# Counts in the sort, edge weights in groups of 64 rows, attributes four quads ahead, and root products inside the relational loops

## What is computed

```python
def _rgcn_layer(x, src, dst, edge_type, edge_attr, W, root, bias, nn_w, nn_b):
    n = x.shape[0]
    edge_w = edge_attr @ nn_w.T + nn_b          # 53125 x 32 by 32 x 256
    msg = jax.nn.relu(x[src] * edge_w)
    out = x @ root + bias
    for r in range(N_REL):                      # 3 relations
        mask = edge_type == r
        m = jnp.where(mask[:, None], msg, 0.0)
        s = jax.ops.segment_sum(m, dst, num_segments=n)
        cnt = jax.ops.segment_sum(mask.astype(x.dtype), dst, num_segments=n)
        mean = s / jnp.maximum(cnt, 1.0)[:, None]
        out = out + mean @ W[r]
    return out
```

## Time and profile before

| | |
|---|---|
| median of 3 runs | 5542.0 us (5537.71 to 5550.64) |
| the profiled execution | 5537.87 us, span 5536.0 us |
| mean granted TensorE clock | 0.814 of full speed |
| busy: PE, PEld | 3725.7 us (67%), 2918.2 us (53%) |
| busy: DVE, ACT, POOL | 2873.2 us (52%), 1521.7 us (27%), 2684.7 us (48%) |
| sort loop | 24 to 650 us of the span |
| relational loops | 2872 to 3679, 3782 to 4551 and 4663 to 5427 us |
| dense stages | 3679 to 3775, 4555 to 4651 and 5427 to 5516 us |

### The profile page before, as it was taken

How to read it: one execution, slowest core, us unless ns; L and a number is a source line. 1 busy time by engine, 2 the same in 40 slices (tenths; PEclk the granted TensorE clock), 3 DMA queues, 4 the chain that set the end, 5 groups by cost and what they waited for, 6 DMA issues and landing times.

```text
span 5536.0 us, 114152 instructions
## 1 busy us (share of the span) xinstructions
PE 3725.7 (67%) x28769; PEld 2918.2 (53%) x28769; DVE 2873.2 (52%) x10883; ACT 1521.7 (27%) x3922; POOL 2684.7 (48%) x2864
## 2 busy tenths in 40 slices
PE   2212185666666766666658888997778778777778
PEld 1111133444444344444437777876666677666677
DVE  5444454444445544444465555554555554555556
ACT  1000003555554155555522222211222221222220
POOL 5666504555554255555545455424555533555550
PEclk6555587989888899888867888898788889888888
DMA  2111136666665366666632222212222321222220
GB/s 46 22 22 22 21 116 187 174 172 174 170 169 120 104 173 173 171 172 171 167 102 79 77 83 78 80 50 81 81 81 83 85 65 58 84 83 81 81 83 30
DMA packets 375435, 563.79 MB, mean 102 GB/s; under 512 B 133583, under 2 KB 261632, under 8 KB 375362
## 3 DMA queue, kind: packets, MB, share of 16 engines
q0 software_dynamic: 155264, 442.19, 29.5%
q1 hardware_dynamic: 165304, 113.92, 7.3%
q10 hardware_dynamic: 54794, 6.81, 0.8%
HBM read 521.54 MB, written 41.08 MB: 102 GB/s over the span
## 4 chain that ended last, share of the span: by engine, by line
PE 35%; issue 18%; DVE 16%; another core or an unknown queue 16%; DVEq 6%; SPq 4%; DMA 3%; ACT 2%; ACTq 0%; POOL 0%; POOLq 0%
PE bank L1074 10%; PE bank L1089 9%; PE bank L963 5%; PE bank L1030 3%; SPq L783 2%; DVE ht L1640 2%; PE bank L1040 2%; DVE region L1724 2%; DVE ht L1627 1%; PE bank L1013 1%; DVEq L651 1%; PE bank L1056 1%; DVE region L1650 1%; DMA rings<-edge_attr_T 1%
## 5 line engine op out<-in xcount | busy, mean ns | idle before, releaser
L555 POOL DMA_INDIRECT gring<-h_rows,gidx x1248 | 1185.6, 950 | 1078.3 <-DVE rings L1701 734.7
L1089 PE MATMUL bank<-rings 128*128 128x96 f32 x6168 | 1041.5, 314 | 216.8 <-DVE region L1724 142.4
L1074 PE MATMUL bank<-nnwt,rings 128*128 128x256 f32 x3084 | 1001.2, 452 | 218.9 <-DMA rings<-edge_attr_T 153.0
L1089 PEld LDWEIGHTS bank<-rings 128*128 128x128 f32 x6168 | 965.9, 226 | 313.2 <-DVE region L1724 187.5
L1701 DVE TENSOR_TENSOR rings<-bank,gring 128x256 f32<-128x256 f32 x1542 | 583.0, 420 | 952.0 <-remote 417.5
L1156 ACT ACTIVATE rings<-rings 128x512 f32<-128x512 f32 x771 | 485.6, 630 | 1864.0 <-DVE rings L1701 1491.5
L1074 PEld LDWEIGHTS bank<-nnwt,rings 128*128 128x128 f32 x3084 | 626.6, 225 | 311.4 <-DMA rings<-edge_attr_T 145.3
L1030 PE MATMUL bank<-rings 128*64 128x128 f32 x4096 | 393.1, 320 | 541.1 <-ACT rings L1189 202.6
L523 POOL DMA_INDIRECT gring<-kv_rows,gidx x512 | 487.9, 953 | 473.0 <-PE bank L1056 185.4
L523 POOL DMA_INDIRECT ht<-kv_rows,gidx x512 | 493.7, 964 | 417.5 <-PE bank L1056 229.6
L1724 DVE TENSOR_TENSOR region<-region,bank 128x192 f32 x1542 | 539.2, 350 | 123.8 <-issue 27.2
(11 more groups left out here) (245 smaller groups left out, 4702.4 us busy)
## 6 DMA issues: line engine op xcount, KB each, us to landing
rings<-node_in_window_T SPq DMA_DIRECT2D x256, 128.0 KB
rings<-edge_attr_T SPq DMA_DIRECT2D x1548, 16.0 KB
gring<-h_rows,gidx POOLq DMA_INDIRECT x1248
kv_rows<-rows SPq DMA_DIRECT2D x50, 258.0 KB, 2.5
gring<-kv_rows,gidx POOLq DMA_INDIRECT x512
ht<-kv_rows,gidx POOLq DMA_INDIRECT x512
region<-edge_records SPq DMA_DIRECT2D x13, 576.0 KB, 7.0
edge_records<-rings POOLq DMA_INDIRECT x416
```

Of the source, the lines that this page charges most:

```text
L555: g.indirect_dma_start(out=gring_r[:, 2 * u + k, :], out_offset=None, in_=h_d[l], in_offset=bass.IndirectOffsetOnAxis(ap=gidx_r[:, half, 2 ...
L1074: ins = pe.matmul(bank[slot % RL][:, k * D:(k + 1) * D], eat[:, b, 2 * (slot % 2) + k, :], nnwt[:, :], start=True, stop=True)
L1089: ins = pe.matmul(b[:, (2 * k + c) * SEG:(2 * k + c + 1) * SEG], prod[:, slot % RL, (2 * k + c) * P:(2 * k + c + 1) * P], one, start=True, ...
```

## The change

Four edits go together.

1. **Counts in the sort.** `one_hot` makes a second one-hot of the segment (relation and node in the window, 96 wide), and `ranks` multiplies it by the first in four products a group, added up in bank 4 over all 104 groups. The sums by segment and window are the counts. The count products, the adds and `ones_f` leave layer 0.
2. **Edge weights in groups of 64 rows.** The even tile of a pair lies in partitions 0 to 63 of `eat`, the odd in 64 to 127, the weights `nnwt` in both, and each product contracts over its own 64. The four products of a quad are issued together, the two groups in different banks.
3. **Attributes four quads ahead.** `eat` holds four quads (`EB`) in the space of two.
4. **Root products in the loops.** In the first 25 trips of a loop SP fetches a block of rows (`hrow`), PE transposes it (bank 6), ACT copies it, PE multiplies it by the root weights (bank 7) and ACT keeps the result in `rootrows`. The dense stage has six products a block, no transposes and no `copy_features`. The message sums have two banks in place of four (`RS`), and `LAG_RACC` goes from 3 to 2.

```diff
@@ sort: ranks, one_hot
+                for c in range(CG):
+                    pe.matmul(bank[4][0:SEG, 0:NW], onehot_s[:, slot, :, c], onehot_w[:, slot, c, :],
+                              start=isinstance(trip, int) and g + c == 0, stop=isinstance(trip, int) and g == G - 1 and c == CG - 1)
...
-                                iota_w[:, :, :], ALU.is_equal).then_inc(s_ohw, 1)
+                                iota_w[:, :, :], ALU.is_equal)
+                v.tensor_tensor(onehot_s[:, slot, :, :],
+                                own_f[:, bass.ds(g * CG, CG)].unsqueeze(1).to_broadcast([EP, SEG, CG]),
+                                iota_w[:, 0:SEG, :], ALU.is_equal).then_inc(s_ohw, 1)
@@ SP, loop of a layer
+                    if root and u == U_LOAD:
+                        wait_freed(sp, s_turn, l * NT + trip)
+                        sp.dma_start(hrow, h_d[l][bass.ds(trip * P, P), :]).then_inc(s_hrow, 16)
...
-                    wait_freed(sp, s_ew, l * RPAIRS + trip * U + u - 2)
+                    wait_freed(sp, s_ew, l * RQUADS + trip * QTRIPS + quad - EB + 1)
@@ PE, dense stage
-                    for r in range(-1, NREL):
-                        o = bank[b + (r + 1) // 2][:, (r + 1) % 2 * D:((r + 1) % 2 + 1) * D]
+                    for r in range(NREL):
+                        o = bank[b + r // 2][:, r % 2 * D:(r % 2 + 1) * D]
@@ PE, relation_tiles
+                if root and u == U_TURN:
+                    pe.wait_ge(s_hrow, 16 * (l * NT + trip + 1))
+                    wait_freed(pe, s_hturn, l * NT + trip)
+                    for c in range(2):
+                        ins = pe.transpose(bank[6][:, c * P:(c + 1) * P], hrow[:, c * P:(c + 1) * P], ident[:, :])
+                    ins.then_inc(s_turn, 1)
+                if root and u == U_ROOT:
+                    pe.wait_ge(s_hturn, l * NT + trip + 1)
+                    wait_freed(pe, s_root, l * NT + trip)
+                    for c in range(2):
+                        ins = pe.matmul(bank[7][:, 0:D], hturn[:, c, :], wts[:, l % 2, NREL, c, :], start=c == 0, stop=c == 1)
+                    ins.then_inc(s_rootp, 1)
...
-                    wait_freed(pe, s_prod, at + p - RL + 1)
-                    for k in range(2):
-                        ins = pe.matmul(bank[slot % RL][:, k * D:(k + 1) * D], eat[:, b, 2 * (slot % 2) + k, :], nnwt[:, :],
-                                        start=True, stop=True)
+                    wait_freed(pe, s_prod, at + p - 2)
+                    for pair in range(2 if live(trip, u + 1, 0, RPAIRS) else 1):
+                        for k in range(2):
+                            g = slice(k * RG, k * RG + KE)
+                            ins = pe.matmul(bank[2 * b + k][:, pair * D:(pair + 1) * D], eat[g, e, pair, :], nnwt[g, :],
+                                            start=True, stop=True)
...
-                    wait_freed(pe, s_racc, 2 * (at + p - RL + 1))
-                    b = bank[RL + slot % RL]
+                    wait_freed(pe, s_racc, 2 * (at + p - RS + 1))
+                    b = bank[RL + slot % RS]
...
-                        if l == 0:
-                            pe.matmul(b[0:SEG, 4 * SEG + k:4 * SEG + k + 1], one, ones_f[:, :], start=True, stop=True)
@@ DVE, dense stage
-                    v.tensor_tensor(o, bank[b][:, 0:D], bias_r[:, l, :], ALU.add).then_inc(s_dv, 1)
+                    v.tensor_tensor(o, rootrows[:, i, :], bias_r[:, l, :], ALU.add).then_inc(s_dv, 1)
+                    v.wait_ge(s_dn, n + 1)
```

More of the change, by code:

```diff
@@ L49 @@
 RQUADS = -(-RPAIRS // 2)
+QTRIPS = U // 2
+RG = P // 2
+KE = RG
+EB = 4
 HALF = U
@@ L117, in run_steps, with run_root_steps @@
         step(trips, u)
+def run_root_steps(eng, lag, step, trips, blocks):
+    for u in range(U):
+        step(0, u, True)
+    with eng.Fori(1, blocks) as trip:
+        for u in range(U):
+            step(trip, u, True)
+    with eng.Fori(blocks, trips) as trip:
+        for u in range(U):
+            step(trip, u, False)
+    for u in range(lag):
+        step(trips, u, False)
 def tile_of(trip, u, lag):
@@ L232, in build @@
         orow = rows[:, 0:4 * D].rearrange("p (s f) -> p s f", s=4)
+        hrow = rows[:, 0:D]
+        hturn = rows[:, D:2 * D].rearrange("p (c n) -> p c n", c=2)
         assert 4 * D <= 2 * KVW
@@ L623, in gpsimd_program @@
                 else:
[L624 removed]
+                    g.wait_ge(s_jobs, 48)
                 relation_gathers(l)
@@ L833, in ranks @@
                 pe.wait_ge(s_ohw, g + 1)
-                if not isinstance(trip, int):
+                if not isinstance(trip, int) or trip:
                     pe.wait_ge(s_row, ROWSTEPS * (g - GU + 1))
@@ L848, in tensor_program @@
                 ranks(0, slot)
-            with pe.Fori(1, GTRIPS) as trip:
+            with pe.Fori(1, GTRIPS - 1) as trip:
                 for slot in range(GU):
                     ranks(trip, slot)
+            for slot in range(GU):
+                ranks(GTRIPS - 1, slot)
             pe.wait_ge(s_row, ROWSTEPS * G)
@@ L1275, in vector_program @@
             step(v.scalar_tensor_tensor(meta[:, :, 2], int_e[:, :], float(SEG - W), meta[:, :, 2], ALU.mult, ALU.add))
+            step(v.scalar_tensor_tensor(own_f[:, :], typ_e[:, :], float(W), row_e[:, :], ALU.mult, ALU.add))
             v.wait_ge(event("counted"), 2)
@@ L1317, in vector_program @@
                     rows_of(trip, slot)
+            step(v.memset(cnt_t[:, NW:NWP], 0.0))
+            step(v.tensor_copy(cnt_t[:, 0:NW], bank[4][0:SEG, 0:NW]))
+            after()
             tables_of_tiles(v, step, after, tell)
             v.wait_ge(event("nnw"), 1)
-            v.wait_ge(s_small, 16 * 25)
-            tell("nnwt", v.tensor_copy(nnwt[0:ND, :], bank[7][0:ND, 0:D]))
+            v.wait_ge(s_small, 16 * 26)
+            step(v.tensor_scalar(inv_t[:, :, :].rearrange("p r i -> p (r i)"), bank[7][:, D:D + NREL * NT], 1.0, None, ALU.max))
+            after()
+            step(v.reciprocal(inv_t[:, :, :], inv_t[:, :, :]))
+            for g in (0, RG):
+                ins = v.tensor_copy(nnwt[g:g + ND, :], bank[7][0:ND, 0:D])
+            tell("nnwt", ins)
             for l in range(2):
@@ L1700, in step @@
                         row = gring_r[:, bass.ds(place(slot, k), 1), :].rearrange("p o f -> p (o f)")
-                        ins = v.tensor_tensor(prod[:, slot % RL, k * D:(k + 1) * D], bank[slot % RL][:, k * D:(k + 1) * D], row,
+                        weights = bank[slot // 2 % 2 * 2 + k][:, slot % 2 * D:(slot % 2 + 1) * D]
+                        ins = v.tensor_tensor(prod[:, slot % RL, k * D:(k + 1) * D], weights, row,
                                               ALU.mult)
```

179 lines of the change are left out of this document (80 added, 99 removed).

## The result

The changed kernel takes **5592.3 us** (median of 4 runs, 5583.2 to 5599.9) against 5546.3 us for the kernel before on the same chip: ratio 1.0084, 95% interval 1.0069 to 1.0100. It is 0.8% slower, where 6.2% less was forecast. The profiled execution took 5599.9 us (span 5597.9).

A forecast was written before the change was run, and what follows sets the result against it. No engine was full in the loops; several take turns. From 5537.9 us, loops at 680 us each save 300, root products in the dense stages 71, counts in the sort add 30: 5197, called 5195; range 5100 to 5290, chance 0.43.

The forecast's parts named there:

- The lower bound: Attributes four quads ahead: 67 us a loop forecast, bounds 0 and 97; 0 if SP itself is the limit.
- The -41 in layer 0: Layer 0's loop loses two adds a pair on DVE and two products on PE: 41 us saved, bounds 20 and 60.
- The +30 in the sort: Sort: doubled one-hots on DVE and four more PE products a group cost 30 us, bounds 0 and 45.
- Cover exists: Sort: POOL is busiest and DVE idle 268.7 us with no cause named, so added count work is partly hidden.
- the 120.4 us with no cause: Loop 1: DVE's unnamed idle time ahead of its product; might shrink, so 680 us a loop was taken, not 687.
- the 28 and 67 us of PE's and SP's waits: Loop savings summed: 28 us a loop from row groups of 64, 67 from attributes four quads ahead.
- The bursts take it back: Rival: long bursts of POOL's gathers hold DVE and SP, half the loops' gain goes, 730 us a loop, 5347 us; chance 0.22.
- A burst can be no longer than the ring: Argument against the bursts rival: the ring limits how long POOL's run of gathers in the loops can be.
- SP's 611 us: Loop 1: time SP doesn't wait, far over the 323 its issue needs; counted as evidence for the bursts rival.
- Slower: Rival: lag 2 with two banks locks DVE to PE in the loops; 0.55 us a pair, 5620 us; chance 0.06.
- the fourth rival: The slower case: each pair's adds in the loops wait for sums made in the same step; 5620 us, chance 0.06.
- The sign that was to tell the two apart: DVE idle ahead of the adds means lag 2; over 120 us without a cause, with little SP waiting, means bursts.

The follow-up runs named there:

- With breaks: 512-column POOL writes after every second gather of the loops and second scatter of the sort: changed kernel 5116.3 us, kernel before 5152.3 us.
- lag 3: Changed kernel with DVE's adds three steps back again: 5537.0 us, ratio 0.9951; also run with POOL writes between gathers and scatters, ratio 0.9586.

## Why the prediction was wrong

- **Row groups of 64.** Right in kind, the size is better than forecast: 147 us of PE a loop (339 to 192, a factor of 0.57) against 113, the change of mode included, for which 36 more had been set aside. The forecast took 226 us, the undisturbed pace, for the 339 that the loop showed. Its worth was put at 28 us a loop; with the hold shortened it and the attributes together gave nothing.
- **Attributes four quads ahead.** PE's 63 us went, and DVE's 97 us fell to 20 in the whole change and to 79 with this part alone, but the 67 us a loop did not come: 0 alone (1.0012). The lower bound held, for another reason than the one named.
- **Counts.** The -41 in layer 0 came out as some 37, hidden under what all loops lost: layer 0 lost 6 us and the others 46 and 40. The +30 in the sort measured +40, inside its bounds. With breaks the counts cost 2 us, so they cost time where DVE is held. "Cover exists" was right, and the hold took it away.
- **Two banks of sums, lag 2.** Counted +10 a loop, 18 to 21 measured with the hold at full length, 0 or less with breaks; both runs also put the root work into one bank. The wait is not mainly the one worked out (PE too slow in one step): 16 us ahead of the adds name PE and 175 are the late signal, part of which a longer lead hides.
- **Root products.** The dense stages gave 72 us against 71, the part that came as forecast. In the loops the root work costs 0.2 to 0.5 us in 25 trips, 5 to 13 us, against 6 counted.
- **The step that failed** is the one behind the sum: "the 120.4 us with no cause may shrink too when SP and PE are early. I therefore take 680 us a loop". The sum took the 28 and 67 us of PE's and SP's waits as time that leaves the loop, beside an unnamed wait that stays or shrinks. It grew to 236, and the loops took 806 us on average. The experiment with the attributes alone shows the same step by itself: 63 us of PE's wait went, the unnamed wait grew, and the loop kept its length. My reading, which fits the runs but was not tested apart: DVE runs at its own pace until POOL has no break left, and is then held until POOL runs dry, so what is taken from PE's and SP's waits moves into the hold. The rival "The bursts take it back" named the mechanism and let it take half of the gain; it took all of it, and the lag some 20 us a loop more. "A burst can be no longer than the ring" was counted against it, but runs of six to eight gathers, half a ring, are enough to hold DVE 3 to 7 us. "SP's 611 us" was counted too high: 48.8 us more of SP's time in loop 1 of the kernel before are a wait with no cause named.
- **Slower** came true at the place that the fourth rival named, the adds, and at (6 + 46 + 40) / 3 = 31 us a loop. Its cause, a lock of DVE to PE at lag 2, is 18 to 21 of these with the hold at full length and nothing with breaks; by that rival's own price (0.55 us a pair) it would have been 141. The sign that was to tell the two apart did not: the idle time stood ahead of the adds, which was to mean lag 2, and it had no cause named, which was to mean the bursts.

## What to carry to other kernels

A wait "with no cause named" that ends when another engine falls quiet is not one item among others that may be left in the sum. Find what ends it first, because work removed elsewhere can flow into it whole. Where DVE waits for PE beside long runs of indirect gathers, try rests of 0.5 to 0.7 us on POOL after every one or two of them, and give the signal more steps of lead; but time it on more than one chip. On some, rests took 3.5 and 6.0% off the kernel before (0.9649 and 0.9395). On another, longer rests made a loop 37 us longer, and the changed kernel with rests was 5 and 8% slower than the kernel before.

## What the hardware showed that was not expected

- **The hold.** A semaphore that PE raises at the end of a product was raised, and seen by DVE, up to 8.6 us later (median 6.0 over 44 stalls in loop 1), in runs of POOL's gathers or scatters, while PE took DVE's signal within 0.06 us (add done 3997.50, sums begun 3997.56). SP's register instructions take up to 0.7 us each at such times instead of 0.04. It does not follow the bytes (512 or 1024 a row) and gets shorter with gaps of 0.5 to 0.7 us. The signals of DVE and ACT came 0.01 us after their instructions in the same loop. The Trainium skill, SBUF — State Buffer, Who interferes with whom, knows one way in which DVE and GpSimd stop each other: an exclusive lock on a shared port, held for one instruction. By that rule a hold would end with the gather that began it; here DVE, with no instruction running, stayed out over two and more gathers, and PE's sums need no port of DVE's. The records of the semaphores say that DVE does not wake late: it goes on within 0.3 us of the recorded signal in 39 of the 42 stalls of over 0.9 us ahead of the adds of loop 1 (in the other three the signal has no record). Whether PE sends it late or something delays it on its way is open.
- **It depends on the chip.** The other four chips of the experiments ran the kernel before in 5474 to 5553 us, the fifth in 4240, 23% less, and the two traces taken there, both of the changed kernel with breaks, have no hold. What sets the chips apart is open too.
- **A gather costs POOL its instruction, not its rows:** 0.95 us for 128 rows, 0.90 for 64, and the same 0.95 for half of the bytes.
- **PE's granted clock was lower in the changed loops:** in loop 1 it was 0.83 before, with PE busy 77% of the time, and 0.77 after, with 70%. The busy share alone does not order it: with lag 3 it was 0.75 at 75%. The same number of sums took 356.5 us for L1116 against 323.4, so part of the 147 us saved was paid back there. On the fifth chip, in the changed kernel with breaks, it was 0.91.
